# Sums over the states in state layout, one shared buffer for u and silu(y), four decay tiles, projections moved over the block's edge

## The reference, cut to what matters

```python
x_and_res = x @ W_in.T                      # 256 -> 2 * 512
xp, res = jnp.split(x_and_res, 2, axis=-1)
xc = silu(causal_depthwise_conv(xp, 4 taps) + conv_b)
ssm = xc @ W_x.T                            # B (16), C (16), one column of dt
dt = softplus(dt @ W_dt.T + b_dt)           # one value per token and channel
def step(h, inp):                           # over the 1024 tokens
    A_disc = jnp.exp(A[None, None, :] * dt_t[:, :, None])
    h = A_disc * h + dt_t[:, :, None] * B_t[:, None, :] * xt[:, :, None]
    y_t = jnp.einsum('bed,bd->be', h, C_t) + D * xt
    return (h, y_t)
y = silu(y + res)
return y @ W_out.T
```

## Time and profile before

| what | us |
|---|---|
| median of 3 runs (lowest, highest) | 1610.7 (1607.85, 1612.19) |
| the profiled execution, device time | 1612.57 |
| its span in the trace | 1611.0 |
| setup and block 0's front, to the first scan | 0 to 61.5 |
| the scans of the 8 blocks, first start to last end | 61.5 to 995.7 |
| rest of blocks 6 and 7, weights, routing tables | 995.7 to 1076 |
| experts | 1076 to 1560 |
| combine | 1567 to 1611 |

### The profile page before, as it was taken

One profiled execution on the slowest core, in us unless ns is written; L12 is line 12 of the kernel. 1 busy time (PEld: TensorE's weight loads), 2 busy tenths in 40 slices (PEclk: granted clock), 3 DMA queues, 4 the chain that ended last, 5 costly groups with the idle time before them and its releaser, 6 DMA issues. The chain is left out here.

```text
span 1611.0 us, 29240 instructions
## 1 busy us (share of the span) xinstructions
PE 1336.9 (83%) x8770; PEld 1118.7 (69%) x8771; DVE 1157.4 (72%) x2036; ACT 1041.1 (65%) x1438; POOL 1059.9 (66%) x989
## 2 busy tenths in 40 slices
PE   3598898898798898798887796639999999999970
PEld 1367577576577576576577685439999999999970
DVE  2678888888888888888888687436666666666646
ACT  3798996996996996996996874413333333333334
POOL 0288878778877978877978888344444444444436
PEclk8699899999999899999899798659999999999995
DMA  2032132222222222222212223441343631511108
GB/s 98 14 99 80 63 105 76 76 80 89 92 77 89 85 84 89 92 78 88 89 67 85 90 85 122 131 129 53 107 133 117 199 121 39 160 39 40 33 26 308
DMA packets 85677, 150.12 MB, mean 93 GB/s; under 512 B 11408, under 2 KB 34576, under 8 KB 85584
## 3 DMA queue, kind: packets, MB, share of 16 engines
q1 hardware_dynamic: 70480, 116.91, 22.7%
q0 software_dynamic: 9888, 27.29, 5.1%
q10 hardware_dynamic: 5216, 4.74, 0.9%
HBM read 104.45 MB, written 44.45 MB: 92 GB/s over the span
## 5 line engine op out<-in xcount | busy, mean ns | idle before, releaser
L1019 POOL TENSOR_TENSOR arena<-arena 128x1024 f32<-128x1024 f32 x256 | 611.2, 2394 | 73.0 <-DVE arena L796 61.9
L397 PEld LDWEIGHTS d_ps<-ident,arena 128*128 128x128 f32 x2048 | 257.4, 150 | 203.0 <-DVE arena L796 101.5
L397 PE MATMUL d_ps<-ident,arena 128*128 128x128 f32 x2048 | 337.7, 291 | 73.0 <-DVE arena L796 67.5
L618 ACT ACTIVATE arena<-u_tok,b_tok 128x512 f32<-128x512 f32 x512 | 327.3, 713 | 74.4 <-PE d_ps L397 72.8
L796 DVE TENSOR_TENSOR_SCAN arena<-arena,carry,d_ps 128x512 f32<-128x512 f32 x256 | 320.6, 1271 | 74.2 <-PE d_ps L397 72.9
L796 DVE TENSOR_TENSOR_SCAN arena<-arena,d_ps 128x512 f32<-128x512 f32 x256 | 305.1, 1211 | 79.4 <-PE d_ps L397 67.6
L410 PE MATMUL y_ps<-ident,arena 128*128 128x128 f32 x2048 | 311.0, 282 | 40.6 <-POOL arena L1019 40.6
L410 PEld LDWEIGHTS y_ps<-ident,arena 128*128 128x128 f32 x2048 | 248.7, 147 | 47.3 <-POOL arena L1019 47.3
L1306 ACT ACTIVATE h_t<-ht_ps 128x512 f32<-128x512 f32 x142 | 84.5, 595 | 289.8 <-PE ht_ps L1361 289.8
L629 ACT ACTIVATE arena<-dt,neg_a 128x2048 f32<-128x2048 f32 x128 | 255.4, 1995 | 1.9 <-DVE arena L796 1.3
L1371 PEld LDWEIGHTS y_ps<-arena,h_parts 128*128 128x128 f32 x1704 | 214.4, 192 | 8.8 <-issue 4.0
(11 more groups left out here) (170 smaller groups left out, 1681.9 us busy)
## 6 DMA issues: line engine op xcount, KB each, us to landing
arena<-c_rows SPq DMA_DIRECT2D x128, 256.0 KB, 3.4
weight_parts<-arena SPq DMA_DIRECT2D x80, 256.0 KB, 3.8
arena<-weight_parts SPq DMA_DIRECT2D x20, 1024.0 KB, 5.3
arena<-in_pieces SPq DMA_DIRECT2D x80, 128.0 KB, 3.6
xg<-expert_rows POOLq DMA_DIRECT2D x71, 130.0 KB, 2.4
arena<-expert_out SPq DMA_DIRECT2D x16, 512.0 KB, 10.4
arena<-in_pieces SPq DMA_DIRECT2D x12, 512.0 KB, 7.2
x_t<-in_x_t SPq DMA_DIRECT2D x8, 512.0 KB, 5.5
```

Of the source, the lines that this page charges most:

```text
L397: last = nc.tensor.matmul(d_ps[:, c % 2, j * P:(j + 1) * P], ub[:, g % U_RING, j, c * P:(c + 1) * P], t.ident[:], start=True, stop=True, i ...
L618: nc.scalar.activation(ub[:, g % U_RING, j, :], u_tok[:, j, :], ACT.Identity, scale=b_tok[:, b % 2, j, n:n + 1]).then_inc(scaled, 1)
L1019: nc.gpsimd.tensor_tensor(h[:, g % H_RING, lo:hi, :], h[:, g % H_RING, lo:hi, :], c_row[:, g % C_RING:g % C_RING + 1, :].broadcast_to([P, ...
```

## The change

- **Sums in state layout.** `sum_states` issues per quarter one matmul with the identity as the stationary operand and 512 tokens of the state tile as the moving one, in place of four transposes. y then stands in `y_ps` with channels on the partitions. Gate and skip are turned the same way: the gate is still eight 512-wide matmuls per block, the skip becomes four 512-wide ones in place of sixteen 128-wide ones. `turn_y` and its copies (L483, L680) are gone; the output projection reads silu(y) itself, `ys`, which is made in two halves of 256 tokens.
- **Buffers.** u and silu(y) share one tile (`ys`), `tmp` is gone, and there are four decay tiles in place of three; `decays` runs three steps ahead, `scale` still two.
- **Order.** The input projections of channel groups 2 and 3 move from (14, 3) to (15, 2) to (0, 0), (0, 1), (1, 1), (1, 2) of the next block, those of groups 0 and 1 from steps 10 and 11 to step 14; their taps move with them. u is turned in steps 11 and 13 in place of 12 to 14. silu(y) and silu come in step 3 in place of 2, the projection to B, C and dt in step 4, softplus a step later. The output projection is issued in steps 4 to 6 and 8 to 10, in place of 7 to 10.
- **Weights.** One expert's 16 pieces are split before the first scan, in the state tiles, and stored in four DMAs of 1 MB (`first_part`, `first_rest`); 8 pieces per block remain in place of 10. The first scan waits for these stores.
- **Start.** w_in comes in two halves, x_t on ScalarE's queue; in front of block 0 VectorE makes half of the softplus arguments (`first_sizes`), and the first scale reads the turned u from PSUM (`first_scale`).
- **Router.** The eight one-hot comparisons are one instruction.

The sixteen transposes between silu(y) and the output projection are gone. The core of the diff:

```diff
-D_RING = 3
+D_RING = 4
+DECAY_LEAD = 3
...
-        y_u = sb("y_u", [P, EC, T])
-        tmp = sb("tmp", [P, EC, T])
+
+        ys = sb("ys", [P, EC, T])
+        u = ys
...
-        PIECE_STEPS = (0, 1, 3, 4, 6, 8, 9, 10, 11, 12)
-        PARTED = (EXPERTS - W_RING) * PIECES
+        PIECE_STEPS = (0, 1, 3, 4, 6, 8, 10, 12)
+        PARTED = (EXPERTS - W_RING - 1) * PIECES
...
                 def sum_states(b, k):
-                    n, q = divmod(k, 4)
-                    g, half = STATE * b + n, q // 2
-                    pe.wait_ge(hc_done, 2 * g + half + 1)
+                    n, c = divmod(k, 4)
+                    g = STATE * b + n
+                    pe.wait_ge(hc_done, 2 * g + c // 2 + 1)
                     if k == 0 and b > 0:
-                        pe.wait_ge(ys_done, b)
-                    for j in (2 * (q % 2), 2 * (q % 2) + 1):
-                        for c in (2 * half, 2 * half + 1):
-                            last = nc.tensor.matmul(y_ps[:, j, c * P:(c + 1) * P],
-                                                    h[:, g % H_RING, c, j * P:(j + 1) * P], t.ident[:],
-                                                    start=(n == 0 and c == 0), stop=(n == STATE - 1 and c == EC - 1),
-                                                    is_transpose=True)
-                    if q == 3:
+                        pe.wait_ge(ys_done, 2 * b)
+                    last = nc.tensor.matmul(y_ps[:, c, :], t.ident[:], h[:, g % H_RING, c, :],
+                                            start=(n == 0), stop=(n == STATE - 1))
+                    if c == 3:
                         last.then_inc(sum_done, 1)
...
                     if front:
-                        if at == (12, 3):
-                            turn_u(0)
-                        if at == (13, 3):
-                            turn_u(1)
-                        if at in ((14, 0), (14, 1)):
+                        if at in ((11, 2), (11, 3)):
+                            turn_u(q - 2)
+                        if at in ((13, 0), (13, 1)):
                             turn_u(2 + q)
                     if early:
-                        if at in ((14, 3), (15, 0)):
-                            in_projection(2, 0 if n == 14 else 1)
-                        if at in ((15, 1), (15, 2)):
-                            in_projection(3, q - 1)
+                        if at in ((14, 0), (14, 1)):
+                            in_projection(e, 0, q)
+                        if at in ((14, 2), (14, 3)):
+                            in_projection(e, 1, q - 2)
...
                 def y_silu():
                     act.wait_ge(sum_done, STATE * (r + 1))
-                    nc.scalar.activation(y_u[:], y_ps[:], ACT.Silu).then_inc(ys_done, 1)
+                    if r >= 1:
+                        wait_filled(act, "out1", r - 1)
+                    for lo in (0, T // 2):
+                        nc.scalar.activation(ys[:, :, lo:lo + T // 2], y_ps[:, :, lo:lo + T // 2], ACT.Silu)\
+                            .then_inc(ys_done, 1)
...
                     if c == 0:
+                        if g == 0:
+                            dve.wait_ge(first_stored, 16 * FIRST_PARTS)
                         dve.wait_ge(decay_done, g + 1)
```

More of the change, by code:

```diff
@@ L82, in _ @@
         def _(act):
+            for dst, src in early:
+                act.dma_start(dst, src).then_inc(t.first_loaded, 16)
             for dst, src in taps:
@@ L258, in mamba @@
         w_low = sem("w_low")
+        first_raw = [sem(f"first_raw{m}") for m in range(4)]
+        first_high = sem("first_high")
+        first_low = sem("first_low")
+        first_stored = sem("first_stored")
         high_done = sem("high_done")
@@ L421, in gate, with skip @@
                         last.then_inc(gates_done, 1)
-                def skip(j):
-                    for c in range(EC):
-                        nc.tensor.matmul(y_ps[:, j, c * P:(c + 1) * P], xc[:, i % 2, c, j * P:(j + 1) * P],
-                                         t.diag_d[:, c, :], start=False, stop=False)
-                def in_projection(c, k):
+                def skip(c):
+                    nc.tensor.matmul(y_ps[:, c, :], t.diag_d[:, c, :], xc[:, i % 2, c, :], start=False, stop=False)
@@ L465, in spread_z, with spread_z2 @@
                         .then_inc(m_filled[bank_of("z", f)], 1)
+                def spread_z2():
+                    wait_bank(pe, "z2", f)
+                    nc.tensor.matmul(bank("z2", f), t.ones[2 * STATE:2 * STATE + 1, :],
+                                     ssm[2 * STATE:2 * STATE + 1, :], start=True, stop=True)\
+                        .then_inc(m_filled[bank_of("z2", f)], 1)
                 def turn_u(j):
@@ L552, in between @@
[L552 to L557 removed]
+                        m = 4 * (n - 4) + q - 1
+                        if 0 <= m < 8 and n < 7:
+                            out_projection(0, m, m + 1)
+                    if front and at == (5, 3):
+                        spread_z()
+                        if f == 0:
+                            spread_z2()
@@ L619, in scale, with first_scale @@
                                          scale=b_tok[:, b % 2, j, n:n + 1]).then_inc(scaled, 1)
+            def first_scale(j):
+                wait_filled(act, f"ut{j}", 0)
+                nc.scalar.activation(ub[:, 0, j, :], bank(f"ut{j}", 0), ACT.Identity,
+                                     scale=b_tok[:, 0, j, 0:1]).then_inc(scaled, 1)
             def decays(g):
@@ L771, in step @@
                         ut_out(1)
-                    if back and n == 14:
-                        normed()
                     if early and n == 15:
-                        xp_out(2)
-                        xp_out(3)
-            act.wait_ge(t.rest_loaded, 16 * REST_LOADS)
-            nc.scalar.activation(t.neg_a[:], t.neg_a[:], ACT.Exp).then_inc(exp_done, 1)
+                        xp_out(e, 0)
+                        xp_out(e, 1)
             iterations(act, step)
@@ L1117, in step @@
                         times_c(g - 1, 1)
+                    if front and f % 2 == 1 and n == 2:
+                        halo_sums()
+                    if front and f % 2 == 1 and n == 3:
+                        halo_fix()
+                    if place and n == 8:
+                        router_den()
+                    if place and n == 9:
+                        router_spread()
+                    if place and n == 10:
+                        router_weigh()
                     if scans:
```

320 lines of the change are left out of this document (183 added, 137 removed).

## The result

The changed kernel takes **1738.3 us** (median of 4 runs, 1732.7 to 1740.9), the kernel before 1610.0 us (1607.9 to 1612.2): ratio 1.0792, 95% interval 1.0758 to 1.0826, so 8% slower. The prediction said 1697 us and slower, with 1640 to 1742 as range. Sign, mechanism and range held; the middle is 41 us too low. The time lies 4 us inside the upper end of the range, and not in the stretch that got the main chance (1670 to 1730, 0.58) but in the one of "more waits" (1730 to 1770, 0.13).

What follows compares the result with a forecast made beforehand. Four nearly equally loaded engines before, PE after: 901 us of PE work plus waits makes a 1031 us body, +97. With start 0 and tail -11, 1612.6 becomes 1698.6, median 1697 us; range 1640 to 1742.

Steps and rivals of the forecast that it cites:

- more waits: Rival, body: as many uncounted waits as the 66 us of the kernel before; body 1097 us, time 1765; chance 0.13.
- the price of a sum: Each quarter's sum on PE: 0.86 us as one 512-wide matmul for 0.435 as four transposes, +27.2 us per full block.
- The rival of cheap sums: Sums on PE cost less than the gate's 0.86 us; at 0.435 us each the time is 1580 us; chance 0.05.
- PE's work, 117.3 us per full block: Blocks 2 to 5: 92 us of PE work before the change, +27.2 for sums, -1.7 for turn_y, -0.2 for skips.
- The waits, 17 us per full block: PE's standstill in each full block: 10 + 3 + 2 + 1.5 = 16.5 us, 17 with hand-overs, bounds 4 and 25.
- light stretch: Quarters (1, 2) to (3, 3), without sums: PE idles some 6 us, plus some 2.5 us waiting for group 3's copy.
- bank 0 at the edge: Projection of group 2 at (0, 0) waits some 1.5 us for bank 0, freed by DVE's last tap at (15, 3).
- DVE's halves of dt and u: Steps 9 to 11: DVE needs 13.5 us from (10, 1) to (11, 1), so the turn of u waits 3 us.
- third turn of u: At (13, 0) PE waits 2 us for the bank that ScalarE frees behind a scale and a decay.
- What the change takes away is worth little: Body: the removed 21.2 us bank wait at step 11's input projection and fewer copies and weight pieces, booked at nothing.
- The tail: Behind the last scan: turns and copies gone, output projection sooner; -11 us, bounds -4 and -15.
- The better overlap: Rival, body: PE and DVE level out within a step of four quarters; body 985 us, time 1652; chance 0.2.

Runs made afterwards that it cites:

- e6: e4 with every drive of the ten quarters (1, 2) to (3, 3), which have no sums, issued twice: 1710.6 us.
- e4: The changed kernel with ScalarE's copy of channel group 3 at the end of step 1 instead of step 2: 1719.8 us.
- e7: e4 with ScalarE's copies of the first two turned tiles of u between scale and decay of step 13 instead of behind the decay: 1702.8 us.
- e8: The kernel before with only the input projection of channel group 1 moved from (11, 1), (11, 2) to (11, 3), (12, 1): 1587.6 us.
- e11: e2 with the input projection of channel group 1 moved to (11, 3), (12, 1), as in e8: 1664.5 us.
- e2: The kernel before with sums, gate and skip in state layout and no turn of y, all else as before: 1679.4 us in one run.
- e5: e4 with own expert weights split in steps 6 to 13 and the last block's rows of x loaded ahead of most of those weights: 1710.2 us.
- e12: e11 with silu at step 3 instead of 2 and the projection to B, C and dt and its followers a step later; silu(y) stays: 1701.0 us.

## Why the prediction was right, and where it was too low

The profiled execution was forecast at 1698.6 us and took 1740.8. The 42.2 us between them are 37.5 in the body, 6.6 behind it, and -1.9 ahead of it.

- **What bounds the kernel, and the price of a sum:** right, to the digit (0.86 us, two records; 1024 of them). The rival of cheap sums is out: it needed a sum of less than 0.65 us. The prediction sets a granted clock of 0.93 beside three quarters of transposes among PE's records; in e6 the clock of step 3 rose from 0.50 to 0.94, and that of the body from 0.95 to 0.98, with nothing added but transposes.
- **PE's work, 117.3 us per full block:** right. In steps 5 to 12 and 14 the mean of blocks 2 to 5 is 78.0 us (scan starts), and the work of these steps by the prediction's prices is about 76.
- **The waits, 17 us per full block:** 20.3 us measured (138.5 less 118.2, which is the work added step by step). Term by term, as measured length less PE's work:

| term | booked | measured |
|---|---|---|
| light stretch and its clock, steps 1 to 4 | 8.5 + 1.5 | 35.3 - 21.9 = 13.4 |
| bank 0 at the edge, steps 15 and 0 | 1.5 | 15.1 - 13.8 = 1.3 |
| DVE's halves of dt and u, steps 9 to 11 | 3 | 24.8 - 23.4 = 1.4 |
| third turn of u, step 13 | 2 | 10.0 - 6.1 = 3.9 |

  **The terms that were too small are two.** The copy of group 3: booked 2.5 us as a wait of VectorE; it is a chain over a bank to PE's turn for the router, 5.4 us long. With the copy early, step 2 is 2.0 us shorter and the turn still waits 3.6 us, behind taps and scans (e4); this second part stood nowhere in the prediction. And the turn of u: the length of the wait was right, the lower clock behind it (0.83 over the step) was left out (e7). The last 1.5 us in the prediction's 10 + 3 + 2 + 1.5, for the clock, were the author's estimate, and no run shows them as a term. What the runs showed in their place: the lower level (0.50) holds for 136.5 us of the body (0.936 over 1068.8 us), no less than before (133.1), although PE is busier, and with 34.1 us of it left in place of 104.9 the body was 5.7 us shorter (e6 against e4).
- **Blocks 0, 1, 6, 7:** booked 121, 130.3, 130.8 and 112; measured 133.0, 132.5, 135.0 and 114.2. Block 0 has the largest miss, +12: there the two copies of groups 2 and 3 hold up the taps by 4.0 and 3.1 us (DVE's timeline), and PE, without sums to do, is often at the lower level (granted clock 0.88 over the block).
- **"What the change takes away is worth little":** wrong in the old kernel, where the bank wait was worth 22 us (e8), and wrong in size under the new load (16.6 us of body, e11 against the single run of e2). It did not spoil the sum, since the sum was made of what is there afterwards.
- **The start**, 59.6 us for 61.5: within its bounds. **The tail**, -4.4 for -11: the turns and copies did go, but the load of the last rows came too late. With it mended, -9.6 more (e5). The prediction named SP's queue nowhere in this term.
- **The rival "more waits than I count"** came true in part: 38 of its 66 us. The better overlap did not: steps 5 to 12 are as long as PE's work, neither shorter nor longer.

The body's +134.5 us as a chain of runs: state layout of the sums +71.6 (before to e2); bank wait removed -16.6 (to e11); the rest of the change but for its two late copies +44.0 (to e7); copies of u behind the decay +13.9 (e7 to e4); copy of group 3 in step 2 +21.7 (e4 to after, with 6.7 of it in step 13). That the chain closes shows nothing, since each run starts from the one before.

The +44.0 are the open part. By the scan starts 21.3 us of them lie in steps 3 and 4, where silu and the projection to B, C and dt came a step later, and 21.7 in steps 1 and 2, where the input projection of group 3 and its taps now stand ahead of the router's turn; the other steps add up to 1. e12 makes the first part plausible, but its +36.8 is not this part's price: 35.2 us of it lie in steps 3 and 4, against 21.3. The second part is the rival that e12's expectation named, the input projections at the block's edge. No run moves them alone, so their price is not shown.

## What to carry to other kernels

Where one engine is the bound, count its work per stretch, not per block: work moved out of a stretch in which the engine idles into one in which it is full is added time, even if the total is unchanged (in block 0 of e12 3.9 us of projection were moved and the block grew by 4.5). A wait of that engine is priced by its length and by what follows (a wait of 2.0 us cost 1.7 us with the clock at 1.00 behind it and 3.4 us with the fall, e7), so follow each shared bank one use further than the edit. A part of a change that removes a wait should be tried alone on the old kernel: here one moved line (e8) was worth 1.4%, while the change that held it cost 8%.

## What the runs showed of the hardware beyond the expected

The fall of the granted clock from 1.00 to 0.50 came in two places: behind a wait, with the engine at work again, and within one. After 2.0 us of idle PE began at full price (717.84 to 718.27, 0.43 us, clock 1.00) and fell to 0.85 us for each four transposes from 719.53 to 721.23 (0.50 in 719.50:721.00). In the wait of 4.98 us in the kernel before the clock was 1.00 in 606.01:608.00 and 0.51 in 608.00:610.99, and the first projection behind it took 1.86 us at 0.50. The fall didn't come each time: behind the wait of 2.0 us it came in six of seven blocks of the kernel after (0.83 over the step) and in two of seven of e4; in the others the clock was 1.00 over the step. For an engine without slack the wait cost 3.4 us with it and 1.7 without (e7). And full busy time alone says little of the rate: in e4's step 3 PE is busy in 7.62 of 7.82 us, at a granted clock of 0.50.
